# Output stage of a cross-attention and mixture-of-experts kernel: the stores of the sums and of the normalized rows move from SyncE's DMA queue to ScalarE's

## What is computed

```python
x = x + xattn(layernorm(x), ctx, Wq, Wk, Wv, Wo)   # 16 heads, 4 key/value heads, head size 96
x = x + ffn(layernorm(x), W_gate, b_gate, W_e, b_e)

def xattn(latents, context, ...):
    hidden = concatenate([context, latents], axis=1)
    ...
    return out @ Wo.T                                # out: [rows, 1536]

def ffn(x, W_gate, b_gate, W_e, b_e):                # 8 experts, the best 2 of each row
    _, top_idx = top_k(x @ W_gate + b_gate, 2)
    y_all = relu(einsum('bsd,edh->bseh', x, W_e) + b_e)
    return take_along_axis(y_all, top_idx[..., None], axis=2).mean(axis=2)
```

## Time and profile before

| | |
|---|---|
| time, median of 3 runs | 3384.92 us (3384.07 to 3386.4) |
| the profiled execution: its span | 3388.4 us |
| PE busy | 3341.6 us, 99% of the span |
| DVE, ACT, POOL busy | 61%, 49%, 31% |
| instructions | 64330 |
| output stage, from the first matmul of tile 1 to the last of tile 13 | 3075.95 to 3215.2 us |

### The profile page before, as it was taken

The page is one execution under the profiler, slowest core; times in us unless marked ns, Lnnn a source line. Parts: engine busy times, 40 slices in busy tenths (PEclk is TensorE's granted clock), DMA queues, the critical chain, the costliest instruction groups (busy, mean ns, idle before and its releaser), DMA issues. The chain is left out here.

```text
span 3388.4 us, 64330 instructions
## 1 busy us (share of the span) xinstructions
PE 3341.6 (99%) x21610; PEld 3107.7 (92%) x21610; DVE 2052.6 (61%) x2995; ACT 1648.8 (49%) x3146; POOL 1051.4 (31%) x865
## 2 busy tenths in 40 slices
PE   8999999999999999999999999999999999998989
PEld 8989999999999999999999999999999999997777
DVE  5346666666666666666666666666666666665645
ACT  3225555555555555555555555555555555552232
POOL 0032223332333333332222222233323333326554
PEclk9999999999999999999999999999999999999989
DMA  6542222222212122222222222222222121226865
GB/s 229 198 144 59 59 65 65 65 61 61 63 46 60 56 63 65 64 65 64 65 65 59 65 57 60 65 65 65 61 61 61 47 61 55 63 75 164 195 194 188
DMA packets 307512, 282.96 MB, mean 84 GB/s; under 512 B 200634, under 2 KB 257546, under 8 KB 307338
## 3 DMA queue, kind: packets, MB, share of 16 engines
q1 hardware_dynamic: 301738, 266.10, 27.6%
q0 software_dynamic: 5728, 16.27, 1.5%
HBM read 208.33 MB, written 73.96 MB: 83 GB/s over the span
## 5 line engine op out<-in xcount | busy, mean ns | idle before, releaser
L822 PE MATMUL ps_proj<-wv_hi,parts 128*125 128x384 f32 x3072 | 875.6, 339 | 0.0
L767 DVE TENSOR_TENSOR probs_lo<-probs,probs_hi 125x448 fp32r<-125x448 f32 (+1 forms) x896 | 682.0, 778 | 275.7 <-ACT probs_hi L694 263.2
L809 PE MATMUL ps_proj<-parts,wk_hi 128*128 128x500 f32 x2304 | 711.1, 390 | 2.9 <-DVEq L722 2.9
L822 PEld LDWEIGHTS ps_proj<-wv_hi,parts 128*125 128x125 f32 x3072 | 560.0, 185 | 5.8
L147 POOL TENSOR_SCALAR parts<-raw 128x1000 fp32r<-128x1000 f32 (+1 forms) x198 | 238.3, 1204 | 957.2 <-PE ps_proj L822 777.8
L686 ACT ACTIVATE probs<-ps_scores 125x448 f32<-125x448 f32 (+1 forms) x896 | 463.0, 517 | 121.6 <-PE ps_scores L870 78.8
L822 PE MATMUL ps_proj<-wv_lo,parts 128*125 128x384 f32 x1536 | 518.4, 338 | 0.0
L809 PEld LDWEIGHTS ps_proj<-parts,wk_hi 128*128 128x128 f32 x2304 | 431.4, 188 | 91.6 <-DVEq L722 3.2
L673 ACT CAST values_hi<-ps_proj 125x384 fp32r<-125x384 f32 x384 | 184.4, 480 | 645.3 <-PE ps_proj L822 645.3
L694 ACT CAST probs_hi<-probs 125x448 fp32r<-125x448 f32 (+1 forms) x896 | 484.1, 540 | 28.3
L736 DVE TENSOR_TENSOR values_lo<-ps_proj,values_hi 125x384 fp32r<-125x384 f32 x384 | 214.3, 558 | 431.6 <-ACT values_hi L673 428.9
(11 more groups left out here) (218 smaller groups left out, 5822.7 us busy)
## 6 DMA issues: line engine op xcount, KB each, us to landing
raw<-in_ctx SPq DMA_DIRECT2D x192, 500.0 KB, 3.6
qk_hi<-proj_out_hi SPq DMA_DIRECT2D x60, 224.0 KB, 2.0
qk_lo<-proj_out_lo SPq DMA_DIRECT2D x60, 224.0 KB, 2.4
queries_hi<-qk_hi SPq DMA_DIRECT2D x32, 336.0 KB, 3.5
queries_lo<-qk_lo SPq DMA_DIRECT2D x32, 336.0 KB, 3.6
att_raw<-attended SPq DMA_DIRECT2D x128, 84.0 KB
probs<-att_raw SPq DMA_DIRECT2D x31, 336.0 KB, 5.7
probs<-inverse_sums SPq DMA_DIRECT2D x31, 336.0 KB, 3.0
```

Of the source, the lines that this page charges most:

```text
L767: dve.tensor_tensor(prs[1][0:R, u % PRING, 0:N], pr[0:R, u % PRING, 0:N], f(prs[0][0:R, u % PRING, 0:N]), ALU.subtract).then_inc(p_lo, 1)
L809: mm = pe.matmul(pproj[n % 2][:, 0:CS], w["wk"][a][:, j // 3, i * P:(i + 1) * P], ct[v][:, c, j // 3, :], start=(j == 0), stop=(j == 3 * K ...
L822: mm = pe.matmul(pproj[n % 2][0:VT, 0:KD], ct[a][:, t // VTC, j // 3, s], w["wv"][v][:, j // 3, :], start=(j == 0), stop=(j == 3 * KT - 1))
```

## The change

The two stores of a tile become two functions, and ACT calls them for tiles 0 to 12. It asks for the store of the sum right behind the root, and for the store of the normalized rows behind the split of tile t+2 and ahead of the copy into `xt`. SP no longer calls them in its loop; its loads stay where they are. The stores of the last tile's normalized rows stay with SP in `experts`.

```diff
@@ combine, SP's loop
                         load(t + 2)
-                    if t > 0:
-                        store_rows(sp, g, scratch, t - 1)
                     if t == 0:
                         store_att(sp, stream, scratch, B - 1, home)
@@ combine, ACT's loop
                 for t in range(OT - 1):
                     deviation(act, g, t)
+                    if t < OS:
+                        store_sum(act, g, scratch, t)
                     if t + 2 < OT:
                         split(t + 2)
+                    store_normed(act, g, scratch, t)
                     if t < OS:
                         turn(t)
@@
-def store_rows(sp, g, scratch, t):
-
-    if t < OS:
-        sp.wait_ge(g["x1_done"], t + 1)
-        sp.dma_start(scratch["x1"][t], g["x1"][:, t % 2]).then_inc(g["x1_stored"][t % 2], 16)
-    sp.wait_ge(g["normed"], t + 1)
+def store_sum(eng, g, scratch, t):
+
+    eng.wait_ge(g["x1_done"], t + 1)
+    eng.dma_start(scratch["x1"][t], g["x1"][:, t % 2]).then_inc(g["x1_stored"][t % 2], 16)
+
+
+def store_normed(eng, g, scratch, t):
+
+    eng.wait_ge(g["normed"], t + 1)
     rows = scratch["xn"][t * P:(t + 1) * P] if t < OS else scratch["xn_dense"][(t - OS) * P:(t - OS + 1) * P]
-    sp.dma_start(rows, g["xn"][:]).then_inc(g["xn_stored"], 16)
+    eng.dma_start(rows, g["xn"][:]).then_inc(g["xn_stored"], 16)
@@ experts, SP
-                store_rows(sp, g, scratch, OT - 1)
+                store_normed(sp, g, scratch, OT - 1)
```

## The result

The changed kernel takes 3402.17 us, median of 5 runs (3401.28 to 3405.57), where the kernel before took 3384.59 us in 5 runs on the same chip (3380.53 to 3386.40). The ratio is 1.0051, with a 95% interval of 1.0040 to 1.0062: 17.6 us slower. The prediction was 3376.5 us, with 3372 to 3386 as its range, so the sign was wrong.

The account below looks back on a forecast made before the run. PE was taken as the bound, with 8.7 us of gaps in the 140 us output stage and DMA close behind. 9.8 - 0 - 2.6 + 1.2 = 8.4 us off 3384.9 gave 3376.5 us, range 3372 to 3386 (8 in 10).

Parts of the forecast that it names:

- The step that failed: Output stage: off SP's queue the `xn` store lands before DVE's next write, 3 us to spare; PE gets back 9.8 us.
- My 5.3 us for 512 KB at half the rate: Both stores on ACT's queue, served beside SP's at half of 195 GB/s, need 5.3 us from the request of the sums.
- One line for all: Rival: DMA engines are the limit, stores land when the backlog has gone, whoever asks; 0 to -2 us, chance 0.27.
- The loads take the wait over: Rival: attended rows come late in more steps and ACT passes the wait to PE; 4.6 us less, chance 0.13.
- ACT is held by its requests: Rival: slow store requests delay ACT's copy into `xt` for PE; up to 12 us more, chance 0.09.
- break-even of 2.1: On ACT, both store requests taking 2.1 us a step would outweigh the 9.8 us gain; SP's took 1.1.
- PE's gaps and the half clock: Output stage: PE gets back four gaps, 7.6 us, and the slow clock behind the longest, 2.2 us; 9.8 us less.
- ACT's requests: Two store requests a step on ACT, 1.1 us, fit in the copy's 1.3 us of slack; cost 0, at most 22 us.
- Attended rows late: Loads sharing the engines with stores come late in two steps at 1.3 us each; 2.6 us lost, at most 15.6.
- The last scatter: End of stage: late loads start 2.5 us earlier, so POOL's last scatter of row numbers lands earlier; 1.2 us gained.
- the dense store: Tile 12, on ACT with copies behind it: one request of 0.33 us beside the wait for the scatter; costs nothing.
- the forecast's own range: Whole kernel if the forecast holds: 3372.5 us (9.8 + 2.5 gained, nothing lost) to 3378.5 us; chance 0.51.

Follow-up runs that it names:

- e1: Changed kernel, with SP again waiting for `normed` so the expert weights are asked for after the store as before; 3407.36 us, ratio 1.0043 to the kernel before.
- e5: Kernel before, with all 24 of POOL's scatters of row numbers moved behind its loop; 3395.63 us, ratio 1.0040 to the kernel before.
- e6: Changed kernel, with all 24 of POOL's scatters of row numbers moved behind its loop; 3394.19 us, ratio 1.0031 to the kernel before.
- e9: Changed kernel, with POOL's scatters of each tile held until the `xn` store of the next tile has landed; 3390.59 us, ratio 1.0018 to the kernel before.
- e11: Changed kernel, with SP asking for expert weights only once the `xn` store of the tile before has landed; 3398.73 us, ratio 1.0018 to the kernel before.
- e2: Kernel before, all on SP's queue, with the expert weights asked for ahead of the two stores; 3409.10 us, ratio 1.0041 to the kernel before.
- e12: Changed kernel, with SP asking for attended rows and expert weights only when `normed` has come; 3391.53 us, ratio 1.0006 to the kernel before.
- e3: Changed kernel, with only the sums' stores on ACT and the normalized rows' stores back on SP; 3392.84 us, ratio 0.9999 to the kernel before.
- e7: Kernel before, with two `xn` buffers, each with its own semaphore; 3384.26 us, ratio 0.9974 to the kernel before.
- e8: Changed kernel, with two `xn` buffers, each with its own semaphore; 3386.66 us, ratio 0.9982 to the kernel before.

## Why the prediction was wrong

**The step that failed** is "The store of `xn` no longer stands behind the loads of its own step, only behind the store of the sums", and from it "`xn` has landed some 6.3 us after" the sum. The wait was to go from 15.3 us to nothing; it went to 21.7. Two things in it were wrong.

First, I read "no longer behind the loads in one queue" as "ahead of them" or at least "side by side with them". The packets show neither: in tile 2's step SP's queue moved 0.84 MB before the first packet of ACT's. e1 shows the price by itself: the order of requests is as before, the queue is another, and the result is 0.43% slower. In the single queue the store was ahead of the 640 KB of the expert; on a queue of its own nothing keeps it ahead. My 5.3 us for 512 KB at half the rate was not far off the median landing of 6.3 us, but a median doesn't set this time.

Second, the scatters. I had the row in hand: the engines were busy at 132 GB/s while PE stood, and the last scatter took 11.98 us for two columns of 128 numbers. I put both down to backlog, took the rate of the whole stage, 195 GB/s, for the store, and called all but 1.3 of the 14.53 us "queue"; of the changed kernel's 16.4 us over 6 came after the last packet had started. e5 and e6 show that the low rate is the scatters' doing: take them out of the loop and the same bytes go at 203 and 205 GB/s, with PE at full clock. A scatter alone is not enough, though: each slow store of the changed kernel also had a large load asked for just ahead of it, and it is the change that put one there every third tile, the expert's and at the end the late loads. The kernel before had its worst case in tile 2, 14.53 us and 6.6 of the 15.3 us; with 768 KB ahead of the store and the expert's load 0.4 us behind it; two more of its stores took 10.35 and 11.47 us, and DVE's four other waits share 8.7 us. In the changed kernel DVE's waits for the four slow stores, 8.4, 6.1, 3.2 and 3.5 us, are 21.2 of the 21.7. Holding back either of the two, the scatters or the expert's load, gives back two thirds (e9, e11); e2 (the order alone) and e12 say the same of the bytes ahead.

What scatters do to a store is open in part. The Trainium skill, "DMA: Bandwidth & Descriptors", section "Queues, rings and completion order", says that the write which reports a transfer is strongly ordered, and lands only after every earlier write of that DMA engine, across its queues. The landings at 3119.2 and 3119.3, 3158.5 and 3158.7 agree with it, and so do the 6 us between the store's last packet and its report: the report seems to stand behind other writes, the scatter's among them. The same page, "Specifications", says that transfers under 512 bytes make the engine read, modify and write; the scatter's elements have 4 bytes. No run here shows it: in the 6 us at 71 GB/s POOL's queue starts no packet, and over the whole step, 3102 to 3120 us, its packets take 2.0% of the engines' time. No run here has scatters of wider elements, or a store with no report to wait for, so which of the two holds the store, and why a queue of its own ends later than a place in the line by more than the bytes beside it explain, was not tried.

**The rivals.** *One line for all* said that the store lands when the backlog has gone, whoever asks, and is nearest to what happened: SP's queue moved 0.84 MB ahead of the first packet of ACT's, and the store, the expert's load and the scatter all landed at 3119.0 to 3119.3. But it priced the change at 0 to -2 us, because I held the line to be the same; the change also moved the store's place in it, and e2 shows what the place alone costs, 0.41%. *The loads take the wait over*: beside the first split of the stage ACT waited for loads twice, 3.2 and 2.4 us, where it had been once and 1.05 us; small beside 21.7. *ACT is held by its requests* had the right sign and is refuted: each request takes 0.33 us, 0.66 a step against a break-even of 2.1, and the sum's store alone on ACT changes nothing (e3). PE's waits for the copy into `xt` come to 1.4 us.

**The terms of the sum.** PE's gaps and the half clock: -9.8 forecast; measured +11.2 and +3.8. ACT's requests: 0, right to within 1.4 us. Attended rows late: 2.6 forecast; ACT waited 3.2 + 2.4 - 1.05 = 4.6 us more, two steps as I had taken, and what of it reached PE can't be told apart. The last scatter: -1.2 forecast and -1.8 measured, but 2.4 us lost again at the end of the block, since the dense store, which I had put at nothing because it lay "beside the wait for the scatter", is in ACT's order ahead of the late splits. That step's cover had gone: `normed` was late. The value of the wait itself was right: with two buffers (e7) its removal gives 8.8 us, where I had 9.8.

**The range.** The mechanism that decided was the wait's own growth, and I had bounded the removed wait from one side only: "0 (the store lands as late as now) and 9.8". Nothing excluded that it lands later. With the expert's load moved ahead, 640 KB at 195 GB/s are 3.3 us more for the store, on each of the steps that load an expert; that bound alone would have put slower among the rivals with a good chance. The 3378.5 us at the upper end of the forecast's own range has no working in the prediction.

## What to carry to other kernels

When a transfer moves to another queue, write down for every step what was ahead of it, what was beside it, and what is now; taking a wait off an issuing engine also lets everything behind that wait start earlier, and it may be just what the moved transfer will compete with. Look at the slowest landings and not the median where a single buffer waits for each of them, and look for small scattered writes on the same engines. Ask of a late landing whether its bytes or its report are late: the packets by queue tell. If one buffer's store is the wait, a second buffer is worth more than any order of requests: here 0.26% gained against 0.51% lost. The Trainium skill, "Perfetto Trace Analysis", section "DMA Optimizations", says that one engine for inputs and another for outputs may make sense, with loops above all. Here that separation is the change, and it cost 0.51%.

## What the runs showed of the hardware

- A store of 256 KB on ACT's queue landed in 3.9 to 6.0 us with no scatter asked for in the 4 us behind it, in 5.8 to 8.2 us with scatters of 512 bytes asked for from 0.9 us behind it, and in 12.4 to 16.4 us with such scatters behind it and a load of 640 KB or more just ahead (four stores of each kind in the changed kernel); scatters themselves took 3.2 to 12.8 us.
- In the slowest of these the store's last packet had started by 3113 us, and it landed at 3119.2. Without scatters in the loop (e6) the same store landed at most 0.4 us behind its last packet.
- The scatters of twelve tiles cost the stage, up to the sum of tile 10, 12 us in one order of requests and 28 us in another, 8 and 21 us of it by way of one wait for a store (e5 and e6 against the kernels that they come from, and against e7 and e8).
- A transfer asked for on its own queue at the same time as 640 KB on another can land later than one asked for ahead of them in the same queue: for tiles 2 and 5, 18.0 and 14.7 us in e1, 14.53 and 11.47 before, and 0.43% of the whole time. Its first packet can come 5 us behind the request, behind what another queue asked for earlier (0.84 MB in the changed kernel).
- A request of a 256 KB store costs ACT 0.33 us, and the same on SP 0.32 to 0.98 us where it stands in one queue with the loads, in one case 4.43 us (e2).
